# A recommendation tower on one core: pair products, packing and MLP for two tiles at a time

## What is computed

```
e = stack([tbl_f[ids[:, f]] for f in range(50)], axis=1)     # 2048 x 50 x 16
gram = einsum('bid,bjd->bij', e, e)
pairs = gram[:, I_IDX, J_IDX]                                # i < j: 1225 per sample
x = [pairs, dense_ctx]                                       # 1241 inputs
y = relu(relu(x @ W_top1 + b_top1) @ W_top2 + b_top2) @ W_top3
```

## Time and profile before

| | |
|---|---|
| three runs | 724.23, 726.15, 729.40 us; median 726.15 |
| the profiled execution | 728.45 us, of which the trace spans 726.4 |
| mean granted TensorE clock | 0.764 of 2.4 GHz |
| PE busy (matmuls) | 455.6 us, 63% of the span |
| PEld, DVE, POOL, ACT busy | 417.8 (58%), 294.8 (41%), 294.1 (40%), 176.9 us (24%) |
| DMA queue of SP | 52308 packets, 37.01 MB, 16.8% of the 16 DMA engines' time |

### The profile page before, as it was taken

The page is one execution under the profiler, slowest core; times in us unless marked ns, Lnnn a source line. Parts: engine busy times, 40 slices in busy tenths (PEclk is TensorE's granted clock), DMA queues, the critical chain, the costliest instruction groups (busy, mean ns, idle before and its releaser), DMA issues.

```text
span 726.4 us, 21406 instructions
## 1 busy us (share of the span) xinstructions
PE 455.6 (63%) x9792; PEld 417.8 (58%) x9792; DVE 294.8 (41%) x539; ACT 176.9 (24%) x309; POOL 294.1 (40%) x295
## 2 busy tenths in 40 slices
PE   2561354466677656587878556767777683754676
PEld 1451243466666556576767556667667582754676
DVE  2662777345352464434443363352634033033000
ACT  2226211101123232212123321120303422123132
POOL 6676368555444232444444233243445525100000
PEclk9676655556899768978887677679898876766878
DMA  7744221211202212220212222111111110100110
GB/s 261 269 156 159 62 63 28 48 35 19 72 7 72 87 50 48 59 40 11 64 15 70 70 68 44 34 21 28 17 33 21 30 35 12 40 22 24 40 40 2
DMA packets 63338, 41.28 MB, mean 57 GB/s; under 512 B 51328, under 2 KB 57616, under 8 KB 63120
## 3 DMA queue, kind: packets, MB, share of 16 engines
q1 hardware_dynamic: 52308, 37.01, 16.8%
q0 software_dynamic: 9216, 2.38, 4.2%
q10 hardware_dynamic: 1724, 0.52, 0.3%
HBM read 28.81 MB, written 0.14 MB: 40 GB/s over the span
## 4 chain that ended last, share of the span: by engine, by line
PE 39%; issue 16%; SPq 11%; ACT 10%; DVE 9%; another core or an unknown queue 8%; DMA 5%; ACTq 1%; DVEq 0%
PE look_ps L628 18%; SPq L339 11%; PE mlp_ps L657 11%; PE gram_ps L647 6%; PE mlp_ps L680 4%; DVE onehot L436 4%; ACT looked L761 3%; DMA ids_bc<-ids_dram 3%; ACT gram L742 3%; DVE turned L540 2%; ACT split L779 1%; DMA z_both<-gram 1%; ACTq L889 1%; DVE w_sb L594 1%
## 5 line engine op out<-in xcount | busy, mean ns | idle before, releaser
L404 POOL DMA_INDIRECT emb<-tbl,gidx x288 | 293.6, 1019 | 326.3 <-PE gram_ps L647 222.4
L657 PE MATMUL mlp_ps<-z_both,w_sb 127*128 127x128 f16 x2112 | 160.2, 241 | 31.7 <-issue 27.9
L657 PEld LDWEIGHTS mlp_ps<-z_both,w_sb 127*128 127x128 f16 x2112 | 144.5, 109 | 40.7 <-issue 35.0
L628 PE MATMUL look_ps<-parts,onehot 125*128 125x64 f16 x1836 | 90.2, 217 | 110.8 <-DVE onehot L436 48.9
L628 PEld LDWEIGHTS look_ps<-parts,onehot 125*128 125x128 f16 x1836 | 81.2, 114 | 117.2 <-issue 68.3
L436 DVE TENSOR_SCALAR onehot<-ids_bc,rows 125x2048 f16<-125x2048 f16 (+1 forms) x144 | 96.3, 699 | 104.0 <-PE look_ps L628 49.2
L628 PE MATMUL look_ps<-parts_med,onehot 125*128 125x128 f16 x1200 | 96.0, 246 | 36.2 <-DVE onehot L436 17.9
L436 DVE TENSOR_SCALAR onehot<-ids_bc,rows_med 125x1024 f16<-125x1024 f16 x150 | 69.5, 492 | 120.4 <-remote 63.9
L628 PEld LDWEIGHTS look_ps<-parts_med,onehot 125*128 125x128 f16 x1200 | 86.2, 112 | 40.7 <-issue 17.6
L647 PE MATMUL gram_ps<-turned 32*64 32x50 f16 x4096 | 58.3, 214 | 66.3 <-ACT gram L742 42.1
L647 PEld LDWEIGHTS gram_ps<-turned 32*64 32x64 f16 x4096 | 47.1, 121 | 78.3 <-ACT gram L742 44.4
(11 more groups left out here) (39 smaller groups left out, 141.4 us busy)
## 6 DMA issues: line engine op xcount, KB each, us to landing
ids_bc<-ids_dram SPq DMA_DIRECT2D x28, 512.0 KB
emb<-tbl,gidx POOLq DMA_INDIRECT x288
z_both<-gram SPq DMA_DIRECT2D x31, 121.0 KB
z_both<-w SPq DMA_DIRECT2D x1, 2816.0 KB
z_both<-gram SPq DMA_DIRECT2D x31, 90.8 KB
z_both<-gram SPq DMA_DIRECT2D x155, 6.2 KB
z_both<-gram SPq DMA_DIRECT2D x31, 60.5 KB
parts_med<-med SPq DMA_DIRECT2D x2, 800.0 KB
```

The lines of the kernel that those rows point to most:

```text
L404: pool.indirect_dma_start(emb[:, T % TPC, f, :], None, big[f], bass.IndirectOffsetOnAxis(ap=gidx[:, T, f:f + 1], axis=0)).then_inc(gathere ...
L628: last = nc.tensor.matmul(bank[:, half, at:at + width], onehot[0:TP, at_ring, i, t * TILE:(t + 1) * TILE], moving.rearrange("p i s d -> p ...
L657: return nc.tensor.matmul(mlp_ps[n // 2][:, n % 2, :], w1_sb[0:KP, k, w, n * 128:(n + 1) * 128], z_parts[0:KP, T % 2, x, k, :], start=(k = ...
```

## The change

Tiles 0 to 11 are taken in six pairs, tiles 12 to 15 singly (`UNITS`, ten units; `FIRST_SINGLE` = 12, `NP` = 6).

- Pair products of a pair: eight rounds of 32 matmuls with 128 weight columns (64 of each tile) and 100 moving columns (50 of each); only the two 50x50 blocks on the diagonal are used. After a round ACT makes two copies of 50 partitions x 784 elements, one for each tile (before: one of 114 x 784 for each round of 64 matmuls). A single tile keeps four rounds of 64 matmuls, but holds all its samples in one half of the partitions; ACT copies two of the four banks and DVE the other two (`copy_dots` on DVE, new).
- A tile is packed by 9 DMAs of 128-sample (512-byte) runs instead of 18 of 256 bytes; the dense values come once a unit.
- The first, second and third layers of a pair run with 256 columns: 132, 8 and 2 matmuls a pair instead of a tile. `split_products` of a pair takes 2816 elements instead of 1408.
- `turned`, `gram`, `z` and `z_parts` hold one pair, where they held two tiles in turn. So `turn` of a pair's tiles waits for the pair products of the pair before, the first copy of a pair for the packs of the pair before, `pack` for the split of the unit before. `h2` and `y_sb` lie inside `h1`.
- Order: pair products of pair u come in the first half of slot 2u+2, two rounds a position, its packs in the same slot, its split at the end of slot 2u+3, its MLP in slots 2u+4 and 2u+5. Slots run to T = 11 only.
- Last tiles: DVE's order is `split_rows`, `turn`, four half copies, then the split of that same tile. PE puts 13 matmuls of the previous tile's first layer behind each round. The last pack goes to SP (5 pieces) and ACT (4), and the last tile's split and first layer go in two parts (`LAST_KS`).

```diff
+FIRST_SINGLE = NTILES - TPC
+UNITS = [(T, T + 1) for T in range(0, FIRST_SINGLE, TWO)] + [(T,) for T in range(FIRST_SINGLE, NTILES)]
+PER_ROUND = {2: 4, 1: 8}
+ROUNDS = [SPQ // PER_ROUND[len(u)] for u in UNITS]
+def before(u):
+    return u - 1 if u <= NP else u - 2
...
-            for T in range(NTILES):
+            for T in range(FIRST_SINGLE + 1):
                 if T % TPC == 0 and T // TPC + 1 < NCH:
                     load_sample_ids(T // TPC + 1)
...
                 for h in range(2):
                     for o in LOADS_AT[2 * T + h]:
                         load_ids_bc(o)
-                if T >= 1:
-                    pack(T - 1)
-            pack(NTILES - 1, (0,))
+                    if T >= 2 and T % 2 == 0:
+                        pack(T - 2 + h)
+            for T in range(FIRST_SINGLE, NTILES - 1):
+                pack(T)
+            pack(NTILES - 1, PIECES[:PACK_SHARE])
...
-            for T in range((NCH - 1) * TPC, NTILES):
-                split_products(T - 2)
+            for T in range(FIRST_SINGLE, NTILES):
                 split_rows(T)
                 turn(T)
-            split_products(NTILES - 2)
-            split_products(NTILES - 1)
+                for e in range(ROUNDS[-1]):
+                    copy_dots(T, e)
+                if T == FIRST_SINGLE:
+                    split_products(NP - 1)
+                if T < NTILES - 1:
+                    split_products(unit_of(T))
+            for part, ks in enumerate(LAST_KS):
+                split_products(NU - 1, part, ks)
...
+                for i in range(n):
+                    b = n * e + i
+                    for buf in (turned, turned2):
+                        for r in range(Q):
+                            p = slice(32 * r, 32 * r + 32)
+                            last = nc.tensor.matmul(
+                                gram_ps[at, r, i * both * NF:(i + 1) * both * NF],
+                                turned[p, home, b, a:a + both, :].rearrange("p a m -> p (a m)"),
+                                buf[p, home, b, a:a + both, 0:NF],
+                                start=(buf is turned), stop=(buf is turned2))
...
+                act.wait_ge(gram_done, R0[u] + e + 1)
+                for T in UNITS[u]:
+                    out, src = evacuation(T, e, slice(0, Q if u < NP else 2))
+                    last = nc.scalar.activation(out, src, ACT.Copy, scale=1.0 / (SCALE * SCALE))
+                last.then_inc(gram_copied, 1)
```

More of the change, by code:

```diff
@@ L171, with packed_by @@
 PACE = 3
+PACES = 4
+def packed_by(u):
+    inc = {v: PIECE_INC * len(UNITS[v]) for v in range(NU)}
+    return sum(inc[v] for v in range(u + 1) if v % 2 == u % 2)
 def fields_gathered(T):
@@ L393, in pace @@
                     return
-                for e in range(EVACS):
-                    if f == fields[e * len(fields) // EVACS] and EVACS * (T - LAG) + e > 0:
-                        pool.wait_ge(gram_done, EVACS * (T - LAG) + e)
+                u = unit_of(T - LAG)
+                first = R0[u] + (T - LAG - UNITS[u][0]) * ROUNDS[u] // len(UNITS[u])
+                for e in range(PACES):
+                    if f == fields[e * len(fields) // PACES] and first + e > 0:
+                        pool.wait_ge(gram_done, first + e)
             def gathers(T):
@@ new lines, in dots, with first_layer @@
+                last.then_inc(gram_done, 1)
+            def first_layer(u, n, k, p, one_group=True):
+                w, x = ((0, 0), (0, 1), (1, 0))[p]
+                b = columns(u)
+                return nc.tensor.matmul(mlp_ps[n // 2][:, n % 2, b], w1_sb[0:KP, k, w, n * 128:(n + 1) * 128],
+                                        z_parts[0:KP, x, k, b],
+                                        start=(k == 0 and p == 0 and (one_group or n % 2 == 0)),
+                                        stop=(k == ST - 1 and p == 2), skip_group_check=not one_group)
@@ new lines, in _ @@
+            u = NU - 1
+            for part, ks in enumerate(LAST_KS):
+                pe.wait_ge(z_split, u + 1 + part)
+                for n in range(N1):
+                    if part == 0 and n % 2 == 0:
+                        pe.wait_ge(mlp_copied, 4 * u + n // 2 - 1)
+                    for k in range(ks.start, ks.stop):
+                        for p in range(3):
+                            last = first_layer(u, n, k, p, one_group=False)
+                    if part == 1 and n % 2 == 1:
+                        last.then_inc(mlp_done, 1)
@@ L892, in _ @@
-            copy_mlp(NTILES - 2, L3_STEP)
-            split_products(NTILES - 1)
-            for g in range(GROUP_POS):
-                copy_mlp(NTILES - 1, g)
+            for e in range(ROUNDS[NP - 1]):
+                copy_dots(NP - 1, e)
+                copy_mlp(NP - 2, e)
+                move(NCH - 1, e)
+            for q in groups_of(NCH - 1)[ROUNDS[NP - 1]:]:
+                move(NCH - 1, q)
+            for g in range(ROUNDS[NP - 1], GROUP_POS * TWO):
+                copy_mlp(NP - 2, g)
```

367 lines of the change are left out of this document (193 added, 174 removed).

## The result

The changed kernel takes 775.1 us (774.1 to 776.6, four runs), the kernel before 727.8 (724.2 to 729.9, four runs): a ratio of 1.066, interval 1.061 to 1.071. The forecast was 693 us, in a range of 660 to 720. The profiled execution of the changed kernel has a span of 772.7 us.

What follows compares the result with a forecast made beforehand. PE, busiest but a third idle, was taken to bound the kernel. Terms of -27 us took the lookups' end from 560.3 to 533; a last stage of 160 instead of 166.1 gave, after span corrections, 693 us, range 660 to 720.

Steps and rivals of the forecast that it cites:

- What bounds the kernel: Up to the last lookup: PE is the busiest engine but idle a third of its time, so work taken off returns partly.
- New waits of a round, +8: Pair-product rounds wait for ACT's two copies: 0 to 0.3 us exposed in slots, 7 us in the first pair; +8 us.
- The rival "slower": ACT holds up the pair-product rounds: slower from 0.85 us a round on, 740 us at 1.2 us a round; chance 0.08.
- The sample ids, -14.3: Slots 4 and 8: PE's waits of 7.38 and 6.95 us for the sample ids' load go; -14.3 us, bounds 0 to -14.3.
- Wide MLP, -8: MLP at 256 columns saves per-matmul overhead in the four pairs beside lookups; -8 us, bounds -5 to -12.
- fewer PE instructions, -6: Pair products and first layer have 2328 fewer matmuls, so PE's issue idle shrinks; -6 us, between 0 and -18.
- Wide pair products, 0: Rounds of 32 wide matmuls at 25 ns, twice the old one, gain nothing; 0 us, ends -16 and +10.
- Work that leaves the slots, -12: Before the lookups end, one tile's MLP and pair products fewer run: 16.5 us off PE, worth -12 us.
- uneven slots, +5: Even slots hold all pair products, odd slots little beside lookups, where PE waits for DVE; +5 us, bounds 0 and +20.
- The last stage, 160: From the last lookup to the end: 159 or 160 us instead of 166.1; -6, bounds -16 and +6.
- The chances: Whole kernel: expected case 0.6, more than that 0.2, no change 0.12, slower 0.08; faster by over 1% 0.84.
- By the terms' own bounds 675 to 711: Whole kernel: the range of the expected case, 693 us, given by its terms' bounds: 675 to 711 us.

Runs made afterwards that it cites:

- the undisturbed trace: The changed kernel as it is, on another chip, where the kernel before takes 574.1 us: 570.1 us, ratio 0.992.
- the two doses: Changed kernel with PE's round signals passed on through POOL: 596.0 us (1.038); passed on only when the previous round's gathers have landed: 803.5 us (1.098).
- the relay: Changed kernel with PE's round signals passed on by POOL in order with its gathers: 596.0 us (1.038); same edit in the kernel before: 572.9 (0.999).

## Why the prediction was wrong, step by step

- **What bounds the kernel.** Read right as far as it went, but 8% of the chain stood under "another core or an unknown queue", and I passed over it. It was the cost that the change multiplied.
- **The miss in two parts.** Where nothing is late the time is 0.992 of the one before, which by ratio is 722 us and 29 above the forecast: 8 us in the slots (19 won, 27 forecast) and 22 in the last stage (16 lost, 6 won forecast). The late chip adds the rest, 53 us. It costs the kernel before 155 us and the changed one 204 (spans): of these 50 us more, 27 fall in the slots and 23 between the last lookup and the pack of tile 12, where the last pair's rounds are.
- **New waits of a round, +8: the step that failed.** "Exposed 0 to 0.3 us a round" held the round to PE's and ACT's times. In the result a round is 6.6 us from copy to copy, since its signal comes behind the burst of gathers. The six pairs' rounds together exceed those of the undisturbed trace by 161 us. By the two doses made (26 us for 33 of rounds, 23 to 28 for 40) that would be worth some 90 to 125 us, an estimate, but the changed kernel lost only 50 us more than the one before. So either long rounds cost less in the slots than the doses say, or the change saves something else on a late chip; which of the two is open. The rival "slower" had the price (from 0.85 us a round on) but the wrong cause, ACT, so that its sign came true is luck. I asked who ends a round's wait, not what a round sets going: in the slots the old rounds stood 10 us apart in the mean on the late chip and 7 on the other, longer than a burst of gathers (four or five, 1.25 us apart), and the new ones stand 2.8 us apart in the mean where nothing is late.
- **The sample ids, -14.3: right.** DVE's wait for them fell from 24.9 to 4.5 us. On the undisturbed chip PE's idle in slots 4 and 8 was 11.28 and 11.05 us before and is gone, more than all the 19 us the slots won. In the result slot 4 has a wait of another kind: 9.27 us of "issue" ahead of a lookup, while DVE waits 9.85 and 4.83 us for "remote" ahead of the compares.
- **Wide MLP, -8, and fewer PE instructions, -6.** 13 wide matmuls take 1.59 us, 122 ns each, as forecast. The first layer's busy time is 126.4 + 37.1 = 163.5 us, before 160.2 (undisturbed 138.1 against 142.5): +3 and -4. But the second layer fell from 46.0 to 30.4 us (37.3 to 30.1 undisturbed) where I had 0.6 a pair. Both layers together save 12 us of PE's busy time on either chip, what -8 for four pairs makes for six: right in sum, with the shares the wrong way round. The "issue" idle of PE's three main lines from 81 us on is 77.5 us, before 80.9: nothing of the 6. It did not stay where it was, though. In the first layer it fell from 27.9 to 2.1 us, and in pair products it rose from 24.1 to 38.7 and in lookups from 28.9 to 36.7. It goes with gathers, not with the count of instructions.
- **Wide pair products, 0: right at the lower clock, too dear at the higher.** My 12.7 ns for an old matmul came from a row at the lower clock; at the higher an old round of 64 takes 0.69 us. A round of 32 takes 0.85 us at the lower clock, 26.6 ns a matmul (I took 25), and 0.53 at the higher, 16.6 ns. Eight rounds of a pair, new against old, are 6.8 against 6.5 us at the lower clock and 4.2 against 5.5 at the higher. In the result 42.3 + 17.1 us busy stand against 58.3, undisturbed 42.4 against 51.5. The Trainium skill (TensorE: Matmul & The Clock Gate, LDWEIGHTS) has a load cost by its columns. The trace agrees at the lower clock, where twice the columns take twice the time; at the higher they take 1.5 times.
- **Work that leaves the slots, -12, uneven slots, +5.** Undisturbed, the slots won 19 us, where the waits for the sample ids that went are 22. If these count in full, all the other terms, together -13 by the forecast, came to +3. Which of them failed there was not taken apart.
- **The last stage, 160: 204.65.** Of the 44.6 us, 30 stand ahead of the pack of tile 12, with late signals in the rounds of the last pair and of tile 12; undisturbed that item is 51.9, better than the 58 forecast. From 12 to 13 it is 38.0 (39.6 undisturbed) and not 28: DVE splits tile 12's products behind ACT's split at 678.72, which stands behind all of the pair's MLP in ACT's program. I had let the split and the MLP run side by side. The last two intervals are 2.9 us each above 23.7: the 9 DMAs take 7.9 and 8.2 us and not 7.4, DVE's copy of its half takes 0.98 us and not 0.82, and the steps from round to round are 1.8 to 2.8 us and not 1.73 (a single tile's round, now in one half of the partitions, takes 1.05 us at the lower clock, before 0.81). That the rows and transposes stand on the path, as the forecast said, is shown by the 15 us which their move gave back.
- **The chances.** 0.08 for slower was too little. On undisturbed chips the truth was 0.992, by ratio at the very edge of the range of 660 to 720, on the other kind 1.066, far outside it. "By the terms' own bounds 675 to 711" was wrong as a sum: the bounds given, all on one side, reach from some 643 to over 750 us. Even where nothing was late the forecast of 4.6% less was 0.8%: the packs got half as many and the last stage none the shorter.

## What to carry to other kernels

Look at what a step sets going, not only at what it waits for: a signal that releases a burst on another engine makes a loop if the next signal can come late by that burst, and rounds set closer than the burst are then as long as it. Read "unknown" and "remote" shares of the chain as a cost that a change can multiply, before looking at engine times. When work is taken out of slots into a serial end, count each engine's program order there: moving two functions won 15 us, nearly the 16 that the last stage had lost.

## What the runs showed of the hardware

- The same kernel takes 573 or 728 us, by the chip. On the late chips PE has 81 and 78 us of "issue" idle from 81 us on, and its signals come up to 5.2 us late while POOL issues gathers; on the others 2 us, and 1.3 us at most. From the pack of tile 12 on, with no gathers left on the late chips, both kinds take nearly the same time (103.1 and 104.2 us, 116.3 and 118.3). The mean granted clock is lower on the late ones too (0.76 and 0.73 against 0.83 and 0.86), but not from that pack on (0.78 and 0.78, 0.81 and 0.82).
- On a late chip a signal that PE gave 2.4 us before a burst's end arrived about 1.1 us behind it (578.4 given, 581.9 seen, burst's end 580.76).
- POOL passes a semaphore on while earlier gathers still wait in its queue: in the relay five of the seven steps between the last pair's rounds stayed at 2.5 to 3.1 us with gathers 1.25 us apart throughout.
- The 155 us that the kernel before loses on a late chip all fall ahead of that pack. How they divide among PE's "issue" idle, late signals of lookups (DVE alone waits 96.7 us for "remote" from 81 us on) and the clock was not settled.
